# Query and key norms clamped by a maximum over pairs, and the feed-forward normalisation moved from VectorE to ScalarE

## What is computed

```
for i in range(6):
    q, k, v = split(shift_tokens(x) @ Wqkv[i], 3)            # 16 heads of 64
    q = q / max(norm(q), 1e-12) * q_scale[i]                 # the clamp is on this norm
    k = k / max(norm(k), 1e-12) * k_scale[i]
    q, k = rotary(q, k)
    out = softmax(q @ k.T * 8 + window_mask) @ v             # windows of 32 with one before
    x = x + out @ Wo[i]
    t = shift_tokens(x)
    xn = (t - mean(t)) / sqrt(var(t) + 1e-5) * g[i] + b[i]   # the feed-forward normalisation
    a, gate = split(xn @ W1[i] + b1[i], 2)
    x = x + (a * gelu(gate)) @ W2[i] + b2[i]
```

## Time and profile before

| what | value |
|---|---|
| median of 3 runs | 1743.48 us |
| lowest and highest | 1729.58 and 1743.85 us |
| the profiled execution, its own time | 1738.27 us |
| its span in the trace | 1736.5 us |
| mean granted clock of TensorE | 0.967 of full |
| DVE busy | 1360.1 us |
| ACT busy | 1244.8 us |
| POOL busy | 1264.0 us |

### The profile page before, as it was taken

The page is one execution under the profiler, slowest core; times in us unless marked ns, Lnnn a source line. Parts: engine busy times, 40 slices in busy tenths (PEclk is TensorE's granted clock), DMA queues, the critical chain, the costliest instruction groups (busy, mean ns, idle before and its releaser), DMA issues.

```text
span 1736.5 us, 67874 instructions
## 1 busy us (share of the span) xinstructions
PE 1532.5 (88%) x28560; PEld 1223.3 (70%) x28656; DVE 1360.1 (78%) x2564; ACT 1244.8 (72%) x4601; POOL 1264.0 (73%) x1492
## 2 busy tenths in 40 slices
PE   6589989899998899999889998989999989989985
PEld 5367777677777677777667777767777767777774
DVE  4678888878887977877878787787788787887873
ACT  3267868777877777777777777786776777776773
POOL 2378787777877867867767768787778687887770
PEclk8699999999999999999999999999999999999998
DMA  4012211021211111211111212111211112111011
GB/s 120 1 40 57 57 40 52 27 58 33 67 57 35 45 47 45 67 45 47 33 28 57 67 38 60 33 40 46 57 51 47 47 33 57 27 49 45 27 45 31
DMA packets 50878, 80.62 MB, mean 46 GB/s; under 512 B 8947, under 2 KB 16806, under 8 KB 50574
## 3 DMA queue, kind: packets, MB, share of 16 engines
q1 hardware_dynamic: 50574, 76.28, 15.8%
HBM read 18.62 MB, written 1.05 MB: 11 GB/s over the span
## 4 chain that ended last, share of the span: by engine, by line
PE 63%; ACT 12%; DVE 11%; issue 7%; POOL 7%; DMA 0%; SPq 0%; POOLq 0%; DVEq 0%
PE ps L442 9%; PE ps L389 7%; PE ps L396 7%; ACT pr L650 7%; PE ps L412 6%; PE ps L452 6%; PE ps L391 5%; PE ps L390 5%; PE ps L423 4%; PE ps L483 4%; DVE v L956 2%; ACT sq L613 2%; PE ps L406 2%; POOL t L779 2%; POOL t L798 2%
## 5 line engine op out<-in xcount | busy, mean ns | idle before, releaser
L779 POOL TENSOR_TENSOR t<-t 128x512 f32<-128x512 f32 x384 | 486.2, 1279 | 84.2 <-DVE t L951 83.6
L650 ACT ACTIVATE pr<-ps,nmax 128x64 f32<-128x64 f32 x1536 | 460.6, 353 | 0.9 <-DVE nmax L966 0.9
L798 POOL TENSOR_TENSOR t<-t,rn 128x512 f32<-128x512 f32 x384 | 397.6, 1056 | 7.5
L650 ACT ACTIVATION_READ_ACCUMULATOR pr<-ps,nmax 128x1 f32 x1536 | 376.8, 248 | 0.0
L949 DVE TENSOR_TENSOR t<-ps,rope 128x512 f32<-128x512 f32 x384 | 261.6, 681 | 58.1 <-PE ps L396 37.9
L809 POOL TENSOR_TENSOR pr<-pr,rsum 128x512 f32<-128x512 f32 x192 | 200.8, 1046 | 135.1 <-DVE rsum L973 134.4
L389 PE MATMUL ps<-w_hi,xt_hi 128*128 128x512 f32 x576 | 272.7, 473 | 26.7 <-DVE t L951 10.3
L613 ACT ACTIVATE sq<-ps 128x512 f32<-128x512 f32 x384 | 233.3, 622 | 69.9 <-PE ps L391 63.2
L951 DVE TENSOR_TENSOR t<-ps,rope 128x512 f32<-128x512 f32 x384 | 260.7, 679 | 0.0
L931 DVE TENSOR_REDUCE ss<-sq 128x8 f32<-128x512 f32 x384 | 259.2, 675 | 0.7
L390 PE MATMUL ps<-w_lo,xt_hi 128*128 128x512 f32 x576 | 235.0, 408 | 3.0 <-issue 3.0
(11 more groups left out here) (122 smaller groups left out, 2714.0 us busy)
## 6 DMA issues: line engine op xcount, KB each, us to landing
v_win<-v SPq DMA_DIRECT2D x384, 128.0 KB, 2.3
wqkv<-wqkv_in SPq DMA_DIRECT2D x36, 256.0 KB, 3.9
xsh<-xr SPq DMA_DIRECT2D x24, 224.0 KB, 2.6
wo<-wo_in SPq DMA_DIRECT2D x6, 512.0 KB, 3.8
w<-w_in SPq DMA_DIRECT2D x6, 342.0 KB, 4.6
w<-w_in SPq DMA_DIRECT2D x6, 172.5 KB
x<-x_in SPq DMA_DIRECT2D x4, 256.0 KB, 4.1
out<-x SPq DMA_DIRECT2D x4, 256.0 KB, 2.7
```

The costliest lines, as they stand in the source:

```text
L650: i = A(pr[:, c, odd * SPAN:(odd + 1) * SPAN], ps[:, S_BANK[odd], c * SPAN:(c + 1) * SPAN], ACT.Exp, bias=nmax[:, odd, c:c + 1], accum_out ...
L779: G.tensor_tensor(t1[:, c, :], t1[:, c, :], t2[:, c, :], ALU.add).then_inc(qk_added[c], 1)
L798: G.tensor_tensor(w, w, rn[:, par(u), h2, a, :].unsqueeze(2).broadcast_to([P, 8, E]), ALU.mult).then_inc(done, 1)
```

## The change

The clamp. POOL fills every second element of a new buffer `sums` once with 1e-24. `sum_squares` writes its sums into the other elements. `clamp_norm` is now a `tensor_reduce` with the maximum over these pairs, negated, in place of a `tensor_scalar` with maximum and a factor of -0.5. The factor of one half has moved: the rotary tables are halved on the host, the constant of the Newton step is 3 and not 1.5, and the scale of the logarithm is changed to match.

The normalisation. `ffn_normalise` leaves DVE and goes to the very end of ACT's `step`, as four `Identity` activations with a scale and a bias per partition. POOL's `ffn_power` makes the bias, with two more instructions of 128 by 4 elements: the negated mean, and its product with the reciprocal deviation.

The layer boundary. ACT makes the upper parts of V0 and V1 after both groups of exponentials, where one stood between them. POOL's `lower_w` of V1 and `split_w1_values` stand some calls earlier in its `step`, and some waits that others cover are gone or have changed hands.

```diff
@@ constants
-    return rope.astype(np.float32), np.concatenate([band, ident], 1)
+    return (0.5 * rope).astype(np.float32), np.concatenate([band, ident], 1)
@@ ACT
-                    if c in (V0, V1):
+                    if c == V0:
                         act.wait_ge(qkv_ps[c], u + 1)
...
-                A(r, ss[:, par(u)].rearrange("p b a h -> p (b a h)"), ACT.Ln, scale=-2.0 * LN_SHIFT).then_inc(ln_done, 1)
+                A(r, ss[:, par(u)].rearrange("p b a h -> p (b a h)"), ACT.Ln, scale=-LN_SHIFT).then_inc(ln_done, 1)
...
+            def ffn_normalise(f):
+                act.wait_ge(f_rstd, f + 1)
+                for b in range(QUAD):
+                    i = A(xh[:, b, :], xsh[:, b, :], ACT.Identity, scale=rstd[:, f % 2, b:b + 1], bias=shift[:, f % 2, b:b + 1])
+                i.then_inc(f_xh, 1)
...
                 run(s, 1, exps, 0)
-                run(s, 0, upper_w, V1)
                 run(s, 1, exps, 1)
                 run(s, 0, upper_w, V0)
+                run(s, 0, upper_w, V1)
+                run_quad(s, 7, ffn_normalise)
@@ POOL
+            G.memset(sums[:].rearrange("p b a c h k -> p (b a c h) k")[:, :, 1], 1e-24).then_inc(const_ready, 1)
-            G.memset(three_halves[:], 1.5).then_inc(const_ready, 1)
+            G.memset(threes[:], 3.0).then_inc(const_ready, 1)
...
                 G.tensor_scalar(rstd[:, f % 2, :], mv[:, f % 2, :, 1], EPS, None, ALU.add).then_inc(f_sum, 1)
+                G.tensor_scalar(neg_mean[:, f % 2, :], mv[:, f % 2, :, 0], -1.0, None, ALU.mult)
                 pool.wait_ge(f_sum, f + 1)
-                G.tensor_tensor(rstd[:, f % 2, :], rstd[:, f % 2, :], minus_half[:], ALU.pow).then_inc(f_rstd, 1)
+                G.tensor_tensor(rstd[:, f % 2, :], rstd[:, f % 2, :], minus_half[:], ALU.pow).then_inc(f_pow, 1)
+                pool.wait_ge(f_pow, f + 1)
+                G.tensor_tensor(shift[:, f % 2, :], neg_mean[:, f % 2, :], rstd[:, f % 2, :], ALU.mult).then_inc(f_rstd, 1)
...
                 run(s, 2, normalise_k, 1)
+                run(s, 2, lower_w, V1)
                 run(s, 3, normalise_p, 0)
                 run(s, 2, normalise_k, 0)
+                run_layer(s, 6, split_w1_values)
                 run(s, 1, rotate, Q0)
-                run(s, 2, lower_w, V1)
-                run_layer(s, 6, split_w1_values)
@@ DVE
             def sum_squares(u, c):
-                V.tensor_reduce(ss[:, par(u), c // 2, c % 2, :], sq[:, c, :].rearrange("p (h e) -> p h e", h=8), AX.X,
+                V.tensor_reduce(sums[:, par(u), c // 2, c % 2, :, 0], sq[:, c, :].rearrange("p (h e) -> p h e", h=8), AX.X,
                                 ALU.add).then_inc(ss_ready[c], 1)
...
-                w = ss[:, par(u)].rearrange("p b a h -> p (b a h)")
-                V.tensor_scalar(w, w, 1e-24, -0.5, ALU.max, ALU.mult).then_inc(ss_clamped, 1)
+                V.tensor_reduce(ss[:, par(u)].rearrange("p b a h -> p (b a h)"),
+                                sums[:, par(u)].rearrange("p b a h k -> p (b a h) k"), AX.X, ALU.max,
+                                negate=True).then_inc(ss_clamped, 1)
...
-            def ffn_normalise(f):
-                dve.wait_ge(f_rstd, f + 1)
-                for b in range(QUAD):
-                    i = V.scalar_tensor_tensor(out=xh[:, b, :], in0=xsh[:, b, :], scalar=mv[:, f % 2, b, 0:1],
-                                               in1=rstd[:, f % 2, b:b + 1].broadcast_to([P, P]),
-                                               op0=ALU.subtract, op1=ALU.mult)
-                i.then_inc(f_xh, 1)
...
                 run_quad(s, 8, ffn_gated, 0)
-                run_quad(s, 7, ffn_normalise)
                 run_quad(s, 8, ffn_gated, 1)
```

More of the change, by code:

```diff
@@ L97, in build @@
     half_shift = sb("half_shift", [P, 1])
-    three_halves = sb("three_halves", [P, 2 * H])
+    threes = sb("threes", [P, 2 * H])
     minus_half = sb("minus_half", [P, QUAD])
@@ L104, in build @@
     ss = sb("ss", [P, 2, 2, 2, 8])
+    sums = sb("sums", [P, 2, 2, 2, 8, 2])
     rn = sb("rn", [P, 2, 2, 2, 8])
@@ L122, in build @@
     rstd = sb("rstd", [P, 2, QUAD])
+    neg_mean = sb("neg_mean", [P, 2, QUAD])
+    shift = sb("shift", [P, 2, QUAD])
     xsh = sb("xsh", [P, QUAD, P])
@@ L178, in build @@
     newton = sem("newton")
-    f_shifted, f_half, f_stats, f_var, f_sum, f_rstd, f_xh, f_xhT_ps, f_xhT, f_g_ps, f_v_ps, f_gate, f_h, f_y_ps = (
-        sem("f_" + s) for s in ("shifted", "half", "stats", "var", "sum", "rstd", "xh", "xhT_ps", "xhT", "g_ps", "v_ps", "gate", "h", "y_ps"))
+    f_shifted, f_half, f_stats, f_var, f_sum, f_pow, f_rstd, f_xh, f_xhT_ps, f_xhT, f_g_ps, f_v_ps, f_gate, f_h, f_y_ps = (
+        sem("f_" + s) for s in ("shifted", "half", "stats", "var", "sum", "pow", "rstd", "xh", "xhT_ps", "xhT", "g_ps", "v_ps", "gate", "h", "y_ps"))
     c_stats, c_var, c_sum_eps, c_rstd, c_xn, c_tr_ps, c_tr, c_qk_ps, c_qk, c_s_ps, c_max, c_exp, c_sum, c_pn, c_pT_ps, c_pT, c_o_ps, c_x1 = (
@@ L276, in shift_tokens @@
                 else:
-                    sp.wait_ge(const_ready, 9)
+                    sp.wait_ge(const_ready, 10)
                 for t, n in SHIFT_PARTS:
@@ L560, in _ @@
             pe.wait_ge(ld_const, 80)
-            pe.wait_ge(const_ready, 9)
+            pe.wait_ge(const_ready, 10)
             cross_transpose(0)
@@ L698, in step @@
                 run(s, 1, exps, 0)
-                run(s, 0, upper_w, V1)
                 run(s, 1, exps, 1)
                 run(s, 0, upper_w, V0)
+                run(s, 0, upper_w, V1)
+                run_quad(s, 7, ffn_normalise)
             act.wait_ge(ld_const, 80)
             A(ident16[:], ident, ACT.Copy).then_inc(const_ready, 1)
-            act.wait_ge(const_ready, 9)
+            act.wait_ge(const_ready, 10)
             cross_copy_inputs(0)
@@ L772, in lower_w @@
                     w = slice(CHUNK_COLS[c], CHUNK_COLS[c] + 512)
-                    if c in (K0, K1):
-                        pool.wait_ge(w_hi_ready[c], layer_of(u) + 2)
+                    pool.wait_ge(w_hi_ready[c], layer_of(u) + 2)
                     G.tensor_tensor(w_lo[:, w], wqkv[:, w], w_hi[:, w], ALU.subtract).then_inc(w_ready[c], 1)
@@ L788, in refine_norm @@
                 pool.wait_ge(newton, 3 * u + 2)
-                G.tensor_tensor(nt[:], nt[:], three_halves[:], ALU.add).then_inc(newton, 1)
+                G.tensor_tensor(nt[:], nt[:], threes[:], ALU.add).then_inc(newton, 1)
                 pool.wait_ge(newton, 3 * u + 3)
@@ L837, in _ @@
                     split_first_weights(c + 1)
-            pool.wait_ge(const_ready, 9)
             for s in range(FIRST_STEP, LAST_STEP):
@@ L926, in lower_w @@
                     w = slice(CHUNK_COLS[c], CHUNK_COLS[c] + 512)
-                    dve.wait_ge(w_hi_ready[c], layer_of(u) + 2)
+                    if c in (Q0, Q1):
+                        dve.wait_ge(w_hi_ready[c], layer_of(u) + 2)
                     V.tensor_tensor(w_lo[:, w], wqkv[:, w], w_hi[:, w], ALU.subtract).then_inc(w_ready[c], 1)
             def sum_squares(u, c):
-                V.tensor_reduce(ss[:, par(u), c // 2, c % 2, :], sq[:, c, :].rearrange("p (h e) -> p h e", h=8), AX.X,
+                V.tensor_reduce(sums[:, par(u), c // 2, c % 2, :, 0], sq[:, c, :].rearrange("p (h e) -> p h e", h=8), AX.X,
                                 ALU.add).then_inc(ss_ready[c], 1)
@@ L1067, in _ @@
             V.tensor_copy(band16[:], consts[:, 0:SPAN].unsqueeze(1).broadcast_to([P, BLOCKS, SPAN])).then_inc(const_ready, 1)
-            dve.wait_ge(const_ready, 9)
+            dve.wait_ge(const_ready, 10)
             cross_normalise_x(1)
```

## The result

The change is slower. The median is 1821.44 us over 4 runs (1818.33 to 1823.93) against 1739.24 us before, over 4 runs (1729.58 to 1743.85). The ratio is 1.0493, with a 95% interval of 1.045 to 1.0537; the two medians alone give 1.047, which lies inside it. That is 82 us more. The forecast was 1802 us in a range from 1765 to 1838, so the measured time lies in the range and 19 us above the forecast. The profiled execution has a span of 1816.5 us, 80.0 us over the one before.

The account below looks back on a forecast made before the run. No engine is full; the chain that ended last bounds the kernel, 63% on PE. Terms 33 + 13 + 7.5 + 1 + 11 = 65.5 us on the profiled 1738.3 us give 1804 us, stated as 1802 us, range 1765 to 1838.

Parts of the forecast that it names:

- The clamp: DVE's clamp, from 531 ns to about 0.20 us per unit; worth 0 at the end, bounds 0 and -8 us.
- the clock: PE at half clock after its pauses at the transposes: 14 times 0.8 us, 11 us, bounds 0 and 32 us.
- Four activations: The normalisation at the end of ACT's step takes 1.6 us a quad, bounds 0.9 and 2.0 us.
- Form A: 11 quads where the chain runs through ACT's copy and exponentials into Q0's square; 3.0 us each, 33 us.
- Form B: 7 quads where PE, not ACT, is the later one at the transposes; about 1.9 us each, 13 us.
- The slip terms: Delays at the transposes of PE, ACT and DVE from the later normalisation, without half clock: 33, 13, 7.5 and 1 us.
- form C: Five layer boundaries where the chain stays on POOL some 19 us; 7.5 us in all after PE's slack.
- The waits: PE's transposes of `xh` wait for ACT 1.5 to 3.5 us each, 50 to 70 us total, against some 22 before.
- That only the load on ACT stays: PE catches up between quads, leaving ACT's own 1.6 us at 11 quads: 18 us, 1757 us; chance 0.11.
- That the clock falls behind every pause and the boundary slack goes unused: Half clock costs 29 us in place of 11, layer boundaries 19 for 7.5: 1832 us; chance 0.14.
- That DVE's relief decides: Removed DVE work tells in nine quads where DVE reaches the value copies without idling: -18 us, 1720 us; chance 0.05.
- that nothing happens: The new reduction still waits for POOL and the activations fall into ACT's idle time: 1743 us; chance 0.05.

Follow-up runs that it names:

- clamp_only: The kernel before with the clamp as a maximum over pairs (factor of one half moved) as the only change; 1738.27 us against 1738.33, ratio 1.0004.
- boundary_only: The kernel before with only the order at the layer boundaries as in the change; 1736.09 us against 1735.79, ratio 1.0006.
- keep_busy: The changed kernel with twelve unread matmuls more on PE ahead of its wait for the normalised tile; 1793.85 us against 1735.79 before, ratio 1.0336.
- extra_act: The kernel before, normalisation still on DVE, with four unread activations more at the end of ACT's step of each quad; 1757.07 us against 1738.33, ratio 1.0123.
- norm_only: The kernel before with only the normalisation moved to the end of ACT's step and POOL's two extra instructions; 1820.3 us against 1738.33, ratio 1.0493.
- norm_before_guess: The changed kernel with ACT's normalisation moved earlier, ahead of the first guess of the norm; 1738.7 us against 1738.33 before, ratio 1.0007.

## Why the prediction was right, and where it was off

The direction, the place and the kind of the loss were right: the loss is all in the normalisation, PE's transposes wait for ACT at every quad, and ACT waits for the projection behind them. The forecast of 1802 us had 64 us of loss on the profiled time, and 82 us were measured. Without the clock its terms come out nearly right in sum, but partly by luck; the clock was mis-sized. The terms, one by one:

- **The clamp** at 0: right (ratio 1.0004 alone). Its duration, 0.20 us by the line through two reductions, measured 0.220. The Trainium skill, "VectorE: DVE Perf Modes", section "Rules for kernel authors", advises against `tensor_reduce` on a hot path. Here it is the faster form on average, but only beside POOL. The old `tensor_scalar` took 180 to 184 ns in the 21 places where no instruction of POOL ran beside it, but up to 1328 ns elsewhere. The reduction takes 219 to 222 ns at all 96 places:

```profile
L952 DVE TENSOR_REDUCE ss<-sums x96: 219/220/222, 87.0 to 1751.6; 128x32 f32<-128x64 f32 x96
```

- **Four activations** at 1.6 us: they take 1.53 us in the chain. The shortest single one is 477 ns, where I had 491 from the rows and 479 as an estimate from the Trainium skill, "ScalarE: Activation LUTs", section "What ACT_TABLE_LOAD costs". The scale per partition, for which there was no row, was not measured apart; the two operands together add 168 ns to the 309 ns of an activation without them, near the 2 x 91 that I took.
- **Form A** at 3.0 us a quad: quad 16 gives 2.96 us.
- **Form B** at 1.9 us a quad: the waits there are 1.97 to 3.09 us, four of the seven 3.0 or more. PE came late to these transposes before because it ran at half clock (quads 7, 9, 12, 15 and 17) or had paused ahead of them (quads 1 and 22). That is no property of the quad: in clamp_only and boundary_only, which take the same time as the kernel before, the quads whose transposes meet the half clock are 2, 12, 14 and 17, and 9, 10, 15 and 20. In the changed kernel each quad waits some 3.0 us, the boundary ones 2.8 to 4.1.
- **The slip terms in sum.** In keep_busy most of the clock's part is gone, so it shows the slip nearly alone. Over the transposes and the interval behind them, the 11 quads of form A lose 37 us there (forecast 33), six of the seven of form B 6 us (forecast 13 for seven), and the five of form C 3 us (forecast 7.5). Form C loses 20.7 us at the transposes and takes back 17.5 right behind, so there was more slack at the boundaries than I counted. The errors cancel: 1793.85 us is 58 us over the kernel before, where my slip terms (33 + 13 + 7.5 + 1) say 54.5. That is luck in part, and part of the gain behind the transposes may be clock too, since keep_busy has 14 us less of half clock there than the kernel before (by my estimate at most 7 us of time).
- **The clock**, at 14 times 0.8 = 11 us, is the term that was mis-sized. At 21 of the 23 transposes in the steady part PE runs at half clock, at the transposes or within 1.4 us behind their start (all but quads 12 and 16); at quads 9 and 10 the half clock had begun ahead of the pause. Filling the pause brought 28 us, which is 1.3 us for each of the 21. The step that failed is "at most 1.35 us more, and nothing if the low stretch begins behind them, where ACT leads". The first half holds: where the transposes and Q0 run wholly at half clock, the square starts 4.16 us after the start of ACT's first normalisation and not 3.12 (quads 3 and 12, for example), so 1.04 us later. The second half fails. At quad 20 the stretch does begin behind the transposes, and ACT does not lead any more: at half clock PE's projections, transposes and output projection outlast ACT's chain.
- **The waits.** I forecast 50 to 70 us "against some 22 before". Measured are 78.0 us, 69.4 without the last quad. The 22 counts PE's weight loads with the matmuls; of the matmuls alone it was 10.3.
- **The rivals.** That only the load on ACT stays, 18 us: extra_act measures that load as 19 us, and the kernel lost 82, so it is refuted. That the clock falls behind every pause and the boundary slack goes unused, 1832 us: the first is nearly so, the second is not, and the measured 1821 lies between it and the forecast. That DVE's relief decides, or that nothing happens: refuted by clamp_only, norm_only and norm_before_guess.

What stays open is why PE does not come earlier when `copy_o` has moved. The traces show that PE waits for `xh` only at the last quad (8.6 us), and that ACT's wait for PE at the squares has grown; I did not take that further.

## What to carry to other kernels

When work moves to another in-order engine, ask first where in that engine's queue it lands and who waits for it, and only then how busy the engine is: here the same 40 us of activations cost 82 us at the end of the step and nothing a few instructions earlier. Taking work off an engine that waits for others may pay nothing: here DVE lost 66 us of work and the time stayed. A pause of TensorE can be dearer than it looks, since the work behind it may run at half clock; where a pause can't be avoided, matmuls that nobody needs can be worth their place, as the 28 us of keep_busy show.

## What was not expected of the hardware

Of the 23 pauses of 1.97 to 4.13 us ahead of the transposes of the changed kernel, 21 had half clock in them or within 1.4 us behind them, though in two of these it had begun earlier; of the 21 pauses of 1.5 to 2 us in the kernel before, about half had. A pause alone does not settle it: quads 12 and 16, with pauses of 3.01 and 3.05 us, stayed at full clock, and so did two pauses of 2.3 and 2.5 us in keep_busy. The stretch can begin well behind the pause, 1.35 us at quad 20. Twelve extra matmuls in each pause took the half clock from 119.5 to 41.0 us in the stretch from 176 to 1700 us, less than the 54.6 us of the kernel before, and the kernel became 28 us faster.

Of VectorE: in the same place, a `tensor_scalar` on 32 elements mostly ended 0.04 us after an addition of POOL (531 ns on average, 180 without POOL beside it), while a reduction of 64 elements ran beside POOL in 75 of 96 places and never took more than 222 ns. Why one form waits and the other doesn't, no run here shows.
